# One-hots of every second unit in the last batch: made by ScalarE in two passes in place of VectorE

## The chip, the cores and the metric

One NeuronCore of a Trainium2 chip. The metric is the device time of one execution in microseconds (us). Matrix products run on TensorE (PE in the profile; PEld are its weight loads), elementwise work on VectorE (DVE), ScalarE (ACT) and GpSimd (POOL), and SyncE (SP) issues transfers. Each engine runs its own instructions in program order; between engines there are semaphores only.

## The reference, cut to what matters

Two layers over x (4 batches of 512 tokens, 128 features), each a gated cross attention followed by a gated feed-forward. The change lies in the second layer's attention: for each token, 16 heads and 5 taps per head, a position is computed from the token, and the keys and values of a context of 154 entries are read there by linear interpolation:

```python
ix = ((xg + 1.0) * key_len - 1.0) / 2.0
x0 = jnp.floor(ix);  dx = ix - x0;  i0 = x0.astype(jnp.int32);  i1 = i0 + 1
sk = 0.5 * (w0 * _gather_pad0(Kh, i0) + w1 * _gather_pad0(Kh, i1))
sv = 0.5 * (w0 * _gather_pad0(Vh, i0) + w1 * _gather_pad0(Vh, i1))
scores = jnp.einsum('bhqd,bhqkd->bhqk', Qh / math.sqrt(HD), sk)
attn = jax.nn.softmax(scores, axis=-1)
ctx = jnp.einsum('bhqk,bhqkd->bhqd', attn, sv)
```

## The kernel before, in words

The gather is done by matrix products: positions are turned into one-hot matrices, and a table of keys and values (TAB) is multiplied by them. A batch has 20 units, u0 to u19: four quads of four heads, five taps each (a unit is one quad and one tap; `u // 5` is the quad). Batch b's unit u has the running number i = 20 b + u.

For a unit, SyncE's `load_unit` copies the positions of four heads and 512 tokens, repeated over 128 partitions, into one of four slots of `JBM` (512 KB). A slot is loaded anew when TensorE is through with the unit four before (`g_ready`); the load of u+3 is issued in piece G1.u. VectorE's `onehot` compares the slot with the partition's number (0 to 127) and writes 0 or 1 over it: 128x2048 bf16 to fp16, in place (L1054). Context entries above 127 have a second one-hot for a whole quad, `OHR` (L1052), made with the quad's first unit. TensorE then runs 32 and 8 matmuls into a bank of RING (two banks, taken in turn; L949, L954). ScalarE copies the values out (GV, L688), and VectorE, when that is done, multiplies the keys, still in RING, with the queries (prod, L1374); this frees the bank.

The order of all engines is written out by hand in one list of pieces (ORDER); each engine goes through it and takes its part of each piece. In the list a piece is `kind.batch.number`. G0e starts a batch's gather (first loads, first one-hot). In G1.u VectorE makes the one-hot of **u+1** and then the product of u; with u4, u9, u14 and u19 it also sums the quad's products (dots, L1379). G2a, G2b and G2c are the attention: maximum (VectorE), Exp (ScalarE, L701), sum and weights (VectorE from L1400), weighting of GV (VectorE, L1411 to L1416). In batches 0 to 2 they run once behind all units, in the last batch (batch 3) once for each quad, between the units. G3a to G3d are the projections behind a batch's attention: transposes, an eviction by ScalarE (L584) and a product through the one bank MISC, the addition to x by VectorE (L1034), a layer norm (L1017 to L1025), and, for G3d, the store of the batch by SyncE (L491), which is issued when the last addition is done. Batch 2's lie between the units of batch 3:

```
G0e.3 G1.3.0-3 G3a.2 G1.3.4 G2a.3.0 G3b.2 G1.3.5 G2b.3.0 G1.3.6 G2c.3.0 G1.3.7 G3c.2
G1.3.8-9 G2a.3.1 G3d.2 G1.3.10 G2b.3.1 G1.3.11 G2c.3.1 G1.3.12-14 G2a.3.2 G1.3.15
G2b.3.2 G1.3.16 G2c.3.2 G1.3.17-19 G2a.3.3 G2b.3.3 G2c.3.3 Z0.0-1 ...
```

Z0 to Z3 are the last batch's projections and store, in two halves. Before the last gather ScalarE's part of G0e is empty, and its part of G1.u is the copy of GV alone.

Of the kernel before, what the change touches and what calls it, by code (L numbers as in the profile page):

```python
# [8 lines left out]
ALU = mybir.AluOpType  # L9
# [12 lines left out]
NK = 5  # L22
# [64 lines left out]
def build(nc, x, ctxT, mask, maskT, kmask, gates, consts, wq, wk, wv, wo, bq_col, bk_col, rows,  # L87
# [9 lines left out]
    with ctx:  # L97
# [239 lines left out]
        jb_in = [sem(f"jb_in{i}") for i in range(RINGS)]  # L337
        jbr_in = [sem(f"jbr_in{i}") for i in range(2)]
        oh_ready = sem("oh_ready")
        g_ready = sem("g_ready")  # L340
        gv_ready = sem("gv_ready")
        gk_used = sem("gk_used")
# [19 lines left out]
        def of_quad(a, quad, n):  # L362

            return a[:, :, quad * n:(quad + 1) * n]

        def gathered(i, kv):

# [190 lines left out]
        def _(act):  # L558
# [22 lines left out]
            def evacuate(use, dst, src, bias=0.0):  # L581

                act.wait_ge(misc_ready, use + 1)
                act.activation(dst, src, ACT.Identity, bias=bias).then_inc(misc_free, 1)  # L584

            def lower_read(piece):

                if n := before(piece, "F0a"):
                    act.wait_ge(xl_ready, n)

            for piece in schedule:
                kind, b = piece[0], piece[1]
                m = misc_at[piece]
                if kind == "W":

                    act.wait_ge(lg_ready, 1)
                    act.activation(lg[:, 3, :], lg[:, 2, :], ACT.Exp, accum_out=lg1[:, 1:2]).then_inc(act_done, 1)
                    act.wait_ge(act_done, 1)
                    act.activation(lg1[:, 2:3], lg1[:, 1:2], ACT.Ln)
                    act.activation(lg[:, 4, :], lg[:, 1, :], ACT.Ln).then_inc(act_done, 1)  # L600
                    act.wait_ge(act_done, 2)
                    act.activation(lg[:, 5, :], lg[:, 4, :], ACT.Ln, scale=-1.0).then_inc(noise_ready, 1)
                elif kind == "S":

                    e = 3 * b
                    if b == 2:
                        act.wait_ge(w1_ready, 1)
                        act.dma_start(w1f[0], w1[e:e + 3].rearrange("e d i -> d e i")).then_inc(ld_w1[0], 16)
                    act.wait_ge(ld_w1[b % 2], 16 * (b // 2 + 1))
                    act.activation(W1[:, 0, e:e + 3], w1f[b % 2], ACT.Identity, scale=W1SCALE).then_inc(w1h_ready, 1)  # L610
                elif kind == "A0a":
                    lower_read(piece)
                    evacuate(m, xnT[:], MISC[:])
                elif kind == "A0b":
                    if b == 0:
                        load_rest()
                elif kind in ("G0a", "G3a", "G3c"):
                    evacuate(m, QpTs[b], MISC[:])
                elif kind == "A3":

                    f, u = piece[2:]
                    i = b * AU + f * 5 + u
                    act.wait_ge(st_ready, i + 1)
                    if i >= PS:
                        act.wait_ge(pv_done, (i - PS) // 5 + 1)
                    act.activation(PTs[i % PS], RING[:, i % 2, :], ACT.Exp).then_inc(p_ready, 1)  # L626
                elif kind == "A4a":

                    n = b * 4 + piece[2]
                    act.wait_ge(pv_done, n + 1)  # L630
                    if n:
                        act.wait_ge(ctx_ready, n)
                    act.activation(OT[:], SUM[:], ACT.Identity).then_inc(ot_ready, 1)
                elif kind == "A5a":
                    lower_read(piece)
                    evacuate(m, cxT[:], MISC[:])
                elif kind == "F0a":
                    evacuate(m, xnT[:], MISC[:])
                    act.wait_ge(misc_free, m + 1)
                    act.activation(xnTf[:, b % 2, 0], xnT[:], ACT.Identity).then_inc(xh_ready, 1)  # L640
                elif kind == "F0c":

                    act.wait_ge(misc_free, m + 1)
                    act.activation(gt[:, 1], gt[:, 0], ACT.Exp).then_inc(ex_out, 1)
                elif kind == "F0g":
                    act.wait_ge(d_ready, b + 1)
                    act.activation(gs[:, 6], gs[:, 5], ACT.Exp, scale=0.5).then_inc(ex_out, 1)
                elif kind == "F0d":
                    evacuate(m, w9T[:], MISC[0:NE, :])
                elif kind == "F1" and piece[2] < NE:  # L650
                    e, c = piece[2:]
                    if b == 0 and e == 0 and c == 0:

                        act.wait_ge(kparts_out, 64)
                        act.wait_ge(w1_ready, 3)
                        act.wait_ge(ld_moe, 16 * LD_MOE)
                    i = (b * NE + e) * NC + c
                    act.wait_ge(up_ready, i + 1)
                    if i >= HS:
                        act.wait_ge(down_ready, down_count(i - HS))  # L660
                    act.activation(hT[:, i % HS, :], UP[:, i % 2, :], ACT.Silu,  # L661
                                   bias=b1[:, e, c:c + 1], scale=1.0 / W1SCALE).then_inc(h_ready, 1)
                elif kind == "G0b":
                    act.wait_ge(ld_l1, 16 * 5)
                    act.wait_ge(misc_ready, m + 1)
                    for t in range(NT):
                        last = act.activation(Qxs[b][:, t].rearrange("p (h w d) -> p h w d", h=H, w=2),
                                              MISC[:, t * D:(t + 1) * D].rearrange("p (h d) -> p h d", d=DK).unsqueeze(2)
                                              .broadcast_to((128, H, 2, DK)), ACT.Identity)
                    last.then_inc(misc_free, 1)  # L670
                    evacuate(m + 1, QpTs[b], MISC[:], bias=bcol[:, 2:3])
                elif kind == "G0d":
                    if b >= 1:
                        act.wait_ge(j_out, 16 * b)
                        act.wait_ge(jt_out, 16 * NK * b)
                    act.wait_ge(misc_ready, m + 1)
                    act.activation(jT[:], MISC[0:HN, :], ACT.Identity).then_inc(jT_ready, 1)
                    act.wait_ge(jT_ready, b + 1)
                    act.nop().then_inc(misc_free, 1)
                elif kind == "G1":  # L680
                    u = piece[2]
                    i = b * UN + u
                    if u == 0 and b >= 1:

                        act.wait_ge(cx1_ready, b)
                    act.wait_ge(g_ready, i + 1)
                    quad, n = divmod(u, NK)
                    act.activation(GV[:, n, :, quad * 64:(quad + 1) * 64].rearrange("p t (m d) -> p t m d", d=DK),  # L688
                                   gathered(i, 1), ACT.Identity).then_inc(gv_ready, 1)
                elif kind in ("Z0", "Z2"):  # L690
                    n = b + (2 if kind == "Z2" else 0)
                    act.wait_ge(half_turned, n + 1)
                    act.activation(QpTs[B - 1][:, b * 256:(b + 1) * 256], (UP, DOWN)[n // 2][:, b, 0:256],
                                   ACT.Identity).then_inc(half_read, 1)
                elif kind == "G2b":
                    part = piece[2]
                    sc = scs[b].rearrange("p (x h) -> p x h", h=H)
                    if b == B - 1:
                        sc = of_quad(sc, part, 4)
                    act.wait_ge(z_ready, b + part + 1)  # L700
                    act.activation(sc, sc, ACT.Exp, scale=1.0 / math.sqrt(DK)).then_inc(e_ready, 1)  # L701
# [3 lines left out]
        def _(pe):  # L705
# [49 lines left out]
            for piece in schedule:  # L755
# [178 lines left out]
                elif kind == "G1":  # L934
# [4 lines left out]
                    if u == 0:  # L939

                        pe.wait_ge(p_ready, before(piece, "A3"))
                    pe.wait_ge(oh_ready, i + 1)
                    if i >= 2:
                        pe.wait_ge(gk_used, i - 1)
                    o = RING[:, i % 2, :].rearrange("p (t j c) -> p t j c", t=NT, j=NQ)
# [51 lines left out]
        def _(dve):  # L997
# [47 lines left out]
            def onehot(i):  # L1045

                b, u = divmod(i, UN)
                if u % NK == 0:

                    k = i // NK  # L1050
                    dve.wait_ge(jbr_in[k % 2], 64 * (k // 2 + 1))
                    dve.tensor_scalar(OHR[:, k % 2], JBR[:, k % 2], cst[:, C_KR:C_KR + 1], None, ALU.is_equal)  # L1052
                dve.wait_ge(jb_in[i % RINGS], 16 * (i // RINGS + 1))
                dve.tensor_scalar(OHM[:, i % RINGS], JBM[:, i % RINGS], cst[:, C_K0:C_K0 + 1], None,  # L1054
                                  ALU.is_equal).then_inc(oh_ready, 1)
# [503 lines left out]
```

## Time and profile before

| | us |
|---|---|
| median of 3 runs | 831.93 (830.88 to 833.39) |
| the profiled execution | 831.65 |
| its span in the profile | 829.6 |
| busy: PE, DVE, ACT, POOL | 594.7, 487.7, 244.0, 42.7 |

A span is the time from the first to the last instruction of the profile; the execution's time has some 2 us around it. The last batch's gather with its four attentions begins at about 745 us and ends at 817; the last 12.6 us are the Z pieces. In the profile, GV and the Exp of batch 3 are ScalarE's only steady work there; RING is the bank into which a unit's matmuls go, OHA the tile that holds JBM, OHM and OHR, and QAf, in the last batch, the tile of its weights and scores.

### The profile page before, as it was taken

The page shows a single profiled execution, that of the slowest core. Times are in us where ns is not written, and L with a number is a line of the kernel's source. Part 1 is how long each engine was busy: PE and PEld are TensorE (multiplying, and loading weights), DVE is VectorE, ACT ScalarE, POOL GpSimd, SP SyncE. Part 2 cuts the span into 40 slices and gives each one's busy share as a digit, 9 for nine tenths or more (in the row PEclk, how much of TensorE's full clock was granted, in tenths as well). Part 3 has the DMA queues.
Part 4 walks back from the last instruction along what each step waited for, and adds up shares of the span by engine and source line. Part 5 has one row for each costly group of instructions (what it writes and reads, how often), then busy time and mean ns, then how long its engine had stood idle before and what let it go on. Part 6 is the DMA issues. An engine that isn't in the chain of part 4 may idle for free.

```text
span 829.6 us, 14684 instructions
## 1 busy us (share of the span) xinstructions
PE 594.7 (72%) x6038; PEld 418.9 (50%) x6038; DVE 487.7 (59%) x1173; ACT 244.0 (29%) x421; POOL 42.7 (5%) x52
## 2 busy tenths in 40 slices
PE   2256575968998699777777597988759998406563
PEld 1223122635376478653264486854428887405452
DVE  5736664544136635589446545687255475597765
ACT  0001352304555233204434232315335332201110
POOL 1700000000001100000002000000000000000000
PEclk9977696989999889799998897999979999757655
DMA  3390100210000268710000379300002684058440
GB/s 92 62 305 12 50 2 0 50 20 13 1 1 1 50 160 239 214 53 6 0 21 1 72 252 259 132 5 1 13 0 70 207 231 140 1 142 262 111 143 13
DMA packets 40354, 70.71 MB, mean 85 GB/s; under 512 B 9824, under 2 KB 26577, under 8 KB 40097
## 3 DMA queue, kind: packets, MB, share of 16 engines
q1 hardware_dynamic: 30796, 63.64, 27.6%
q10 hardware_dynamic: 9492, 6.14, 2.6%
q8 instruction: 48, 0.79, 0.4%
q14 instruction: 18, 0.14, 0.1%
HBM read 65.82 MB, written 3.95 MB: 84 GB/s over the span
## 4 chain that ended last, share of the span: by engine, by line
PE 49%; DVE 27%; DMA 9%; issue 6%; ACT 5%; SPq 2%; POOL 1%; POOLq 0%; DVEq 0%; ACTq 0%
PE DOWN L750 12%; PE UP L913 9%; PE RING L949 5%; PE RING L954 3%; DMA OHA<-scratch_positions 3%; DVE nmax L1240 3%; PE MISC L715 2%; PE RING L821 2%; DVE xn L1025 2%; PE MISC L724 2%; DMA OHA<-scratch_q_parts 2%; DVE OHA L1054 2%; DMA QAf<-scratch_q_parts 2%; DVE dots L1379 1%; DVE GV L1441 1%
## 5 line engine op out<-in xcount | busy, mean ns | idle before, releaser
L750 PEld LDWEIGHTS DOWN<-W,hT 128*128 128x128 f32 x1152 | 154.1, 197 | 21.9 <-issue 2.6
L750 PE MATMUL DOWN<-W,hT 128*128 128x128 f32 x1152 | 154.8, 280 | 0.2 <-ACT hT L661 0.2
L661 ACT ACTIVATE hT<-UP,b 128x512 f32<-128x512 f32 x144 | 98.3, 687 | 158.9 <-PE UP L913 158.5
L913 PE MATMUL UP<-xnTf,W 128*128 128x512 f16 x432 | 124.3, 403 | 3.4 <-ACT hT L661 3.0
L949 PE MATMUL RING<-TAB,OHA 128*128 128x32 f16 x2560 | 78.8, 180 | 53.6 <-DVE OHA L1054 32.4
L949 PEld LDWEIGHTS RING<-TAB,OHA 128*128 128x128 f16 x2560 | 74.4, 99 | 61.6 <-DVE OHA L1054 39.0
L688 ACT ACTIVATE GV<-RING 128x256 f32<-128x256 f32 x80 | 30.7, 383 | 149.9 <-PE RING L954 149.9
L1070 DVE SCALAR_TENSOR_TENSOR acc<-DOWN,W,acc 128x128 f32<-128x128 f32 x128 | 36.0, 344 | 59.6 <-PE DOWN L750 53.1
L1054 DVE TENSOR_SCALAR OHA<-OHA,cst 128x2048 f16<-128x2048 bf16 x80 | 59.5, 748 | 13.4 <-DMA OHA<-scratch_positions 12.7
L1240 DVE TENSOR_REDUCE nmax<-RING 128x3 f32<-128x462 f32 (+1 forms) x96 | 53.7, 585 | 19.2 <-PE RING L824 15.1
L913 PEld LDWEIGHTS UP<-xnTf,W 128*128 128x128 f16 x432 | 42.4, 103 | 35.2 <-issue 9.5
L954 PE MATMUL RING<-TAB,OHA 128*128 128x128 f16 x640 | 58.8, 247 | 0.0
L1374 DVE TENSOR_TENSOR prod<-RING,Qx 128x256 f32<-128x256 f32 x60 | 25.4, 423 | 53.1 <-ACT GV L688 52.9
L515 POOL TENSOR_TENSOR rstd<-ve,mhalf 128x4 f32<-128x4 f32 x15 | 15.1, 1008 | 717.4 <-DVE ve L1022 717.4
L954 PEld LDWEIGHTS RING<-TAB,OHA 128*128 128x128 f16 x640 | 44.4, 110 | 0.0
L626 ACT ACTIVATE PT<-RING 128x512 f32<-128x512 f32 x54 | 30.9, 600 | 32.0 <-PE SUM L737 15.6
L715 PE MATMUL MISC<-cst,xn 128*128 128x128 f32 x60 | 12.7, 350 | 36.8 <-DVE xn L1025 36.8
L821 PE MATMUL RING<-mb,identb 128*128 128x462 bf16 (+1 forms) x72 | 28.1, 390 | 13.2 <-DVE nmax L1240 7.9
L1025 DVE TENSOR_SCALAR xn<-X,mv,rstd 128x128 f32<-128x128 f32 x60 | 23.0, 558 | 17.0 <-POOL rstd L515 17.0
L715 PEld LDWEIGHTS MISC<-cst,xn 128*128 128x128 f32 x60 | 8.7, 176 | 40.7 <-DVE xn L1025 28.4
L846 PE MATMUL RING<-mbM,identb 128*128 128x512 bf16 x48 | 19.5, 406 | 12.8 <-DMA QAf<-scratch_max_parts 6.8
L824 PE MATMUL RING<-KA,QAf 128*128 128x154 bf16 x192 | 28.0, 254 | 0.0
(321 smaller groups left out, 774.2 us busy)
## 6 DMA issues: line engine op xcount, KB each, us to landing
OHA<-scratch_positions SPq DMA_DIRECT2D x80, 512.0 KB, 5.6
OHA<-scratch_tail_positions SPq DMA_DIRECT2D x48, 160.0 KB, 4.9
OHA<-scratch_positions SPq DMA_DIRECT2D x16, 160.0 KB, 3.9
QAf<-scratch_q_parts SPq DMA_DIRECT2D x18, 128.0 KB
hT<-in_w ACTq DMA_DIRECT2D x3, 768.0 KB, 6.1
W<-in_w ACTq DMA_DIRECT2D x3, 768.0 KB
scratch_q_parts<-qs SPq DMA_DIRECT2D x4, 384.0 KB, 2.5
X<-in_x ACTq DMA_DIRECT2D x4, 256.0 KB, 4.9
```

What stands on the lines that cost most here:

```text
L626: act.activation(PTs[i % PS], RING[:, i % 2, :], ACT.Exp).then_inc(p_ready, 1)
L661: act.activation(hT[:, i % HS, :], UP[:, i % 2, :], ACT.Silu, bias=b1[:, e, c:c + 1], scale=1.0 / W1SCALE).then_inc(h_ready, 1)
L715: last = pe.transpose(MISC[0:width, t * 128:(t + 1) * 128], src[:, t, :], ident)
L750: last = pe.matmul(DOWN[:, n % 2, t * 128:(t + 1) * 128], hT[:, (k + c) % HS, t * 128:(t + 1) * 128], W2[:, e, c, :], start=(c == 0), stop ...
L821: pe.matmul(o, identb[:], mb[:, t, :].unsqueeze(1).broadcast_to((128, n, S2)), start=True, stop=False)
L913: last = pe.matmul(UP[:, i % 2, :], W1[:, pw, e, c * 128:(c + 1) * 128], xnTf[:, b % 2, px], start=(n == 0), stop=(n == 2))
L949: pe.matmul(o[:, t, j, :], OHM[:, i % RINGS, j, t * 128:(t + 1) * 128], TAB[:, b, 0, part, quad * NQ + j, :], start=((j, t, part) == (0, 0 ...
L954: last = pe.matmul(o[:, t], OHR[:, (b * NQ + quad) % 2, n, t * 128:(t + 1) * 128], TAB[:, b, 1, part, quad * NQ:(quad + 1) * NQ, :], start ...
L1025: last = dve.tensor_scalar(xn[:, t, :], X[:, b, t, :], mv[:, t, 0:1], rstd[:, t:t + 1], ALU.subtract, ALU.mult)
L1054: dve.tensor_scalar(OHM[:, i % RINGS], JBM[:, i % RINGS], cst[:, C_K0:C_K0 + 1], None, ALU.is_equal).then_inc(oh_ready, 1)
L1070: last = dve.scalar_tensor_tensor(out=acc[:, t, :], in0=o, scalar=W9[:, b % 2, t, e:e + 1], in1=acc[:, t, :], op0=ALU.mult, op1=ALU.add)
L1240: dve.tensor_reduce(nmax[:, h:h + n, t], RING[:, i % 2, 0:n * S2].rearrange("p (h k) -> p h k", h=n), AX.X, ALU.max, negate=True).then_inc ...
```

## The change

In the last batch the one-hot of the odd units (u1, u3, ... u19) is made by ScalarE, in two passes over the slot, both in place: |k - position|, then max(0, 1 - that), which is 1 where the position is the partition's number and 0 elsewhere. ScalarE makes u1's in G0e.3 and that of u+2 in G1.u, right behind the copy of u's values. VectorE leaves out these units and keeps the tails (`OHR`) of all quads. TensorE waits for ScalarE's count as well as for VectorE's, and for a count of the tails whose unit is ScalarE's (u5, u15).

```diff
+        def on_act(i):
+            return i >= (B - 1) * UN and i % UN % 2 == 1
...
+            def act_onehot(i):
+                n = sum(on_act(k) for k in range(i + 1))
+                act.wait_ge(jb_in[i % RINGS], 16 * (i // RINGS + 1))
+                act.activation(JBM[:, i % RINGS], JBM[:, i % RINGS], ACT.Abs, bias=cst[:, C_K0:C_K0 + 1],
+                               scale=-1.0).then_inc(oh_dist, 1)
+                act.wait_ge(oh_dist, n)
+                act.activation(OHM[:, i % RINGS], JBM[:, i % RINGS], ACT.Relu, bias=1.0, scale=-1.0).then_inc(oh_act, 1)
...
                     act.activation(GV[:, n, :, quad * 64:(quad + 1) * 64].rearrange("p t (m d) -> p t m d", d=DK),
                                    gathered(i, 1), ACT.Identity).then_inc(gv_ready, 1)
+                    if u + 2 < UN and on_act(i + 2):
+                        act_onehot(i + 2)
+                elif kind == "G0e" and b == B - 1:
+                    act_onehot(b * UN + 1)
...
-                    pe.wait_ge(oh_ready, i + 1)
+                    given = sum(on_act(k) for k in range(i + 1))
+                    pe.wait_ge(oh_ready, i + 1 - given)
+                    if given:
+                        pe.wait_ge(oh_act, given)
+                    if tails := sum(on_act(k) for k in range(0, i + 1, NK)):
+                        pe.wait_ge(oh_tail, tails)
...
-                    dve.tensor_scalar(OHR[:, k % 2], JBR[:, k % 2], cst[:, C_KR:C_KR + 1], None, ALU.is_equal)
+                    tail = dve.tensor_scalar(OHR[:, k % 2], JBR[:, k % 2], cst[:, C_KR:C_KR + 1], None, ALU.is_equal)
+                    if on_act(i):
+                        tail.then_inc(oh_tail, 1)
+                if on_act(i):
+                    return
                 dve.wait_ge(jb_in[i % RINGS], 16 * (i // RINGS + 1))
```

## Rows read from the trace of the kernel before

**Rows 1.** Busy time by stretch: engines (instructions), granted clock, DMA share, GB/s.

```profile
740.00:760.00 20.00, 10.52 (x253) 9.75 (x253) 15.83 (x24) 3.16 (x8) 0.00 (x0) 0.76 0.82 252
...
780.00:800.00 20.00, 10.76 (x240) 9.37 (x240) 15.97 (x33) 2.48 (x7) 0.00 (x0) 0.58 0.78 231
```

**Rows 2.** ScalarE's waits, 745 to 817: total us, times, longest.

```profile
ACT GV L688 <- PE RING L954: 57.6, 20, 17.2
```

**Rows 3.** Chain of waits, 744 to 817: start, us; first and last one-hot of seven.

```profile
752.91 0.76 DVE OHA L1054
...
780.68 0.51 SPq L388
...
803.92 0.68 DVE OHA L1054
```

**Rows 4.** ScalarE's instructions grouped by shape, whole execution: busy us, mean ns.

```profile
L584 ACT ACTIVATE QpT<-MISC 128x512 f32<-128x512 f32 x9 | 5.4, 595 | 11.0 <-PE MISC L715 11.0
L610 ACT ACTIVATE W<-hT 128x1536 f16<-128x1536 f32 x3 | 4.3, 1472 | 23.3 <-DMA hT<-in_w 23.3
L701 ACT ACT_TABLE_LOAD x3 | 3.8, 1283 | 0.1
...
L640 ACT ACTIVATE xnTf<-xnT 128x512 f16<-128x512 f32 x4 | 2.5, 630 | 0.1
...
L584 ACT ACTIVATE QpT<-MISC,bcol 128x512 f32<-128x512 f32 x3 | 2.1, 688 | 3.6 <-PE MISC L926 3.6
```

**Rows 5.** DMA issues at 734.8 (u1) and 780.7 us (u13): last number, us to landing.

```profile
OHA<-scratch_positions SPq DMA_DIRECT2D x1, 512.0 KB, 8.3
OHA<-scratch_positions SPq DMA_DIRECT2D x1, 512.0 KB, 5.7
```

**Rows 6.** ScalarE's timeline: GV of u1, u3; G3a's eviction; u4, u5; Exp; u9, u13.

```profile
749.54 0.38 ACT L688 ACTIVATE GV<-RING 128x256 f32<-128x256 f32 x1 [1.14 <-PE RING L954]
...
752.56 0.38 ACT L688 ACTIVATE GV<-RING 128x256 f32<-128x256 f32 x1 [1.07 <-PE RING L954]
753.00 0.60 ACT L584 ACTIVATE QpT<-MISC 128x512 f32<-128x512 f32 x1
755.18 0.38 ACT L688 ACTIVATE GV<-RING 128x256 f32<-128x256 f32 x1 [1.58 <-PE RING L954]
757.54 0.38 ACT L688 ACTIVATE GV<-RING 128x256 f32<-128x256 f32 x1 [1.98 <-PE RING L954]
758.89 0.27 ACT L701 ACTIVATE QAf<-QAf 128x80 f32<-128x80 f32 x1 [0.96 <-DVE QAf L1390]
...
775.74 0.38 ACT L688 ACTIVATE GV<-RING 128x256 f32<-128x256 f32 x1 [1.32 <-PE RING L954]
...
789.66 0.38 ACT L688 ACTIVATE GV<-RING 128x256 f32<-128x256 f32 x1 [3.98 <-PE RING L954]
```

**Rows 7.** TensorE's timeline: first 32 matmuls of u3 and of u13.

```profile
751.10 0.97 PE L949 MATMUL RING<-TAB,OHA 128*128 128x32 f16 x32
...
787.73 1.03 PE L949 MATMUL RING<-TAB,OHA 128*128 128x32 f16 x32 [2.48 <-DVE OHA L1054]
```

**Rows 8.** VectorE's timeline: products of u4, u6, u10, u14, u16 (L1374); sums (L1400).

```profile
755.60 0.42 DVE L1374 TENSOR_TENSOR prod<-RING,QAf 128x256 f32<-128x256 f32 x1
...
760.55 0.28 DVE L1400 TENSOR_REDUCE sm<-QAf 128x16 f32<-128x80 f32 x1
...
762.70 0.42 DVE L1374 TENSOR_TENSOR prod<-RING,QAf 128x256 f32<-128x256 f32 x1
...
780.98 0.42 DVE L1374 TENSOR_TENSOR prod<-RING,QAf 128x256 f32<-128x256 f32 x1
...
793.81 0.42 DVE L1374 TENSOR_TENSOR prod<-RING,QAf 128x256 f32<-128x256 f32 x1 [0.61 <-ACT GV L688]
...
797.97 0.28 DVE L1400 TENSOR_REDUCE sm<-QAf 128x16 f32<-128x80 f32 x1
...
800.12 0.42 DVE L1374 TENSOR_TENSOR prod<-RING,QAf 128x256 f32<-128x256 f32 x1 [0.16 <-ACT GV L688]
```

More of the change, by code:

```diff
@@ L339, in build @@
         oh_ready = sem("oh_ready")
+        oh_tail = sem("oh_tail")
+        oh_dist = sem("oh_dist")
+        oh_act = sem("oh_act")
         g_ready = sem("g_ready")
```

## The prediction, made before the changed kernel ran

> **What bounds the kernel now.** I read the busy time by stretch first, then the chain of waits from 744 us to the end, then ScalarE's waits and the two engines' timelines. All times here are of the one profiled execution: span 829.6 us, 831.65 us as timed. The change touches nothing before the last batch's gather, its 20 units (u0 to u19) between 745 and 809 us and the four quads' attention between them.
>
> In that stretch no engine is full, but VectorE comes nearest: 15.97 of 20 us, against 2.48 for ScalarE and 10.76 for TensorE [rows 1]. ScalarE waits 57.6 us in the gather for TensorE's units [rows 2]. So there is room on ScalarE by the sum. The chain says where time is lost: it runs through VectorE's one-hot, the unit's 40 matmuls, ScalarE's eviction of the values (GV), VectorE's product, then the quad's attention and the next one-hot. Seven of the 20 one-hots are on it, the first and the last at 752.91 and 803.92 [rows 3]. Counting one-hots along VectorE's order, these seven belong to u4, u6, u8, u10, u14, u16 and u18: **every one is an even unit**. The odd units' one-hots, the ones that the change takes off VectorE, run while VectorE would wait for a GV, or for a transfer.
>
> **What goes.** Ten one-hots of 0.68 to 0.76 us [rows 3] leave VectorE: about 7 us of work, and by the chain none of it on the path. I take 0 for it, except in three places where the product behind it becomes early enough to matter once others are late; they are in the steps below.
>
> **What comes.** Ten times two ScalarE passes over 128x2048 16-bit values, in ScalarE's program order. The trace shows no Abs or Relu. Nearest rows, SBUF to SBUF: 128x512 takes 630 ns, 128x1536 takes 1472 ns [rows 4], so 0.82 ns per column and 1472 + 512 x 0.82 = 1.89 us for 2048 columns. A bias held in a column adds 0.09 us (688 against 595 ns [rows 4]): an estimate of 1.98 us for a pass. The ends: 0.75 us, if ScalarE did the tile as fast as VectorE [rows 3], and four times 630 ns = 2.52 us. I take 1.98, since the 1472 ns row is by far the nearest in length and writes 16 bits too. A pair is then 3.95 us from the eviction before to the instruction behind, the passes' small overlaps and the wait between them counted as nothing.
>
> The Trainium skill (ScalarE: Activation LUTs, "What ACT_TABLE_LOAD costs") says that an activation costs the same per element in fp32 and bf16. These rows read fp32 and no row reads 16 bits, so they neither bear it out nor deny it. By its 0.833 ns a column and 280 ns the pass would be an estimate of 1.99 us, and the sum +11; were the rule wrong and 16 bits ran at half the cost, it would be the first rival's 833.3.
>
> **What is behind the pair.** This decides. The pair for u+2 stands behind GV(u), u odd, and ahead of whatever ScalarE does next: GV(u+1), on which VectorE's product of that unit waits, the eviction for batch 2's last projections, and the quads' Exp. Step by step, before -> after:
>
> u1: its load, 8.3 us to land [rows 5], and its passes run while VectorE still weights batch 2. Nothing; otherwise u1's matmuls would start later than u0's end.
>
> u3: GV(1) ends at 749.92 [rows 6], passes to 753.87. TensorE's u3 goes from 751.10 [rows 7] to 753.9. It takes 1.42 us, so GV(3) 752.56 -> 755.36 [rows 6], ends 755.74.
>
> u5: passes to 759.7. Behind them stands the eviction for G3a.2, 753.00 -> 759.7, and behind that GV(4), 755.18 -> 760.3 [rows 6]. The product of u4, 755.60 -> 760.7 [rows 8]: **+5.1**. The same eviction frees MISC for G3b.2, which stands ahead of u5 in TensorE's order, so GV(5) goes from 757.54 [rows 6] to about 763.4 with matmuls at their present rate, 764 if the longer gaps leave TensorE at 1.2 GHz (its granted clock is 0.76 of 2.4 GHz over 740 to 760 us, and 0.58, so mostly the lower level, over 780 to 800 [rows 1]).
>
> u7: passes from 764.0 to about 767.8, and the Exp of quad 0 behind them, 758.89 -> 767.8 [rows 6]. VectorE needs it at its sum of quad 0, 760.55 -> 768.0 [rows 8]; now it had been early. Four instructions later, without u7's one-hot, comes the product of u6, 762.70 -> 769.25 [rows 8]: **+1.45 more, 6.55**.
>
> u9: the load and the passes lie beside quad 0's last sums and the layer norm. Nothing; all of that moves by 6.55.
>
> u11: GV(9) 775.74 [rows 6] + 6.55 ends at 782.7, passes to 786.6, GV(10) 787.0. Product of u10 780.98 -> 787.05 [rows 8], **6.05**: VectorE gets back 0.5 since u11's one-hot stood ahead of that product.
>
> u13: its load is issued behind batch 2's store, at 780.68 [rows 3], 787.25 after, and lands 5.7 us later [rows 5], 792.95. ScalarE stands at it with GV(12) queued behind, passes to 796.9. TensorE's u13 787.73 [rows 7] -> 796.95, and takes 1.9 us (GV(13) at 789.66 [rows 6]).
>
> u15: GV(13) ends 799.25, passes to 803.2, GV(14) behind them to 803.6. Product of u14 793.81 -> 803.6 [rows 8]: **9.8**.
>
> u17: TensorE's u15 803.2 to 805.1, GV(15) to 805.5, passes to 809.45, Exp of quad 2 to 809.75. Its sum 797.97 -> 809.75; the product of u16 800.12 -> 811.0 [rows 8], u17's one-hot being gone from between: **10.9**.
>
> u19: passes end about 815.8, TensorE reaches u19 at 817.4. Nothing. The tail moves as it stands.
>
> **Sum:** 5.1 + 1.45 - 0.5 + 3.75 + 1.1 = +10.9 us. 831.65 + 10.9 = 842.6; the median of before is 831.93, 0.28 above its profile, so 842.8, and I say 843. Twelve passes lie on the path (u3, u5, u7, u13, u15, u17), so 0.1 us a pass is 1.2 us. With 2.52 us a pass it is 10.9 + 12 x 0.54 = +17.4, and some more as u19 is then late too: 850. With 0.75 us the same steps leave only the G3a eviction and GV(4) 0.6 late: 832.5.
>
> **Rivals.**
> 1. 16-bit passes run at half the cost, 1.0 us. Pair 2.05: u3 0.9 late, GV(4) 1.3 late, Exp of quad 0 just in time, u13's passes over at 789.75 and GV(14) no later than the rest. +1.3: 833.3. For: VectorE's one-hot shows that a 16-bit tile can be quick; against: the 16-bit output of the 1472 ns row brought ScalarE nothing visible.
> 2. **Faster.** VectorE is the bound at 80% busy, ScalarE's 57.6 idle us take the pairs, and the released one-hots come off the path: ten of 0.67 us, 831.9 - 6.7 = 825.2. The place is VectorE's order in quads 0 to 2. It decides where a pair is done before GV(u+1) is due; GV(1) and GV(3) are 3.0 us apart [rows 6], so GV(2) is due some 1.5 us behind GV(1), and a pass must stay below about 0.7 us. Against: the chain has no odd one-hot, and 1.98 is far off.
> 3. Abs or Relu needs another table than Exp: a load of 1.28 us [rows 4] to Exp and one back. Exp of quads 0 to 3 would each be 1.28 later, 4 x 1.28 = 5.1, 848. For: no row has Abs or Relu. Against: the Exp line has three loads in the whole execution [rows 4] for its seven Exps, one in each batch before the last and four here, and Identity stands between all of them. The Trainium skill (ScalarE: Activation LUTs, "Table sets: the hidden batching unit") has relu and abs in every set; no run so far shows it. By that rule there is no load, and the sum stays.
> 4. The pairs vanish in ScalarE's idle time and nothing moves: 832. It needs GV(4) and Exp of quad 0 with 4 us of slack; GV(4) has none [rows 8].
>
> **How the numbers follow.** Forecast 0.78, with its own range 838 to 848 (passes of 1.75 to 2.2 us, loads 1 to 2 us off, TensorE's level). Rival 1 0.07, rival 2 0.03, rival 3 0.05, rival 4 0.03; 0.04 for waits longer than I see, above 850. A measurement tells 0.3%, 2.5 us, from no change. Within it are rival 4 and rival 1 but for 0.01 in which that one comes out above 834.4: 0.09. Rival 2 is the faster case, 0.03; the rest is slower, 0.88. The range 836 to 850 holds the forecast and rival 3 and leaves out the rest, 0.17.
>
> **What would show it.** Right: Abs and Relu at about 2 us each; u3's matmuls start behind ScalarE instead of VectorE; the eviction for G3a.2 at about 760; VectorE waits for Exp in quads 0 and 2, some 2 us each; u13's Abs waits for its load; GV ahead of a product becomes VectorE's chief wait; the tail behind the last quad unchanged but some 11 us later. Wrong: passes near 1 us, a table load beside Exp, an odd one-hot's removal that moves a product earlier, or a time below 836.

## The result: slower, and the profile after

The changed kernel takes 847.74 us (842.62 to 851.62) against 831.40 of before on the same chip: a ratio of 1.0178, interval 1.0146 to 1.0211. In a second comparison it took 844.73 against 833.64: 1.0125, interval 1.0076 to 1.0173. That is 16 and 11 us more, where 11 were predicted.

These totals scatter by several us, so the stretch that the change touches is the better measure: from u0's first matmul to the end of quad 3's weighting. Its two ends, before (TensorE's and VectorE's timeline: start, duration, line):

```profile
746.06 1.02 PE L949 MATMUL RING<-TAB,OHA 128*128 128x32 f16 x32 [21.06 <-issue]
...
816.70 0.29 DVE L1416 TENSOR_TENSOR QAf<-GV 128x128 f32<-128x128 f32 x1
```

and after:

```profile
752.11 1.01 PE L974 MATMUL RING<-TAB,OHA 128*128 128x32 f16 x32 [21.06 <-issue]
...
834.81 0.29 DVE L1445 TENSOR_TENSOR QAf<-GV 128x128 f32<-128x128 f32 x1
```

The stretch took 816.99 - 746.06 = **70.93 us** and takes 835.10 - 752.11 = **82.99 us: 12.06 more**. Another 6.05 us of this execution lie ahead of it, where both programs do the same. One piece of that shows between 410 and 445 us: TensorE's granted clock there was 0.95 before, nearly all at 2.4 GHz, and 0.81 after, where it got through 132 matmuls in place of 159 (busy time by stretch, columns as in [rows 1]); before, then after:

```profile
410.00:445.00 35.00, 26.00 (x159) 18.44 (x160) 19.45 (x86) 14.25 (x21) 3.02 (x3) 0.95 0.05 13
```

```profile
410.00:445.00 35.00, 25.05 (x132) 17.22 (x125) 17.52 (x75) 11.96 (x17) 3.02 (x3) 0.81 0.05 13
```

In a second profile of the changed kernel u0 starts at 745.73, as early as before, and the stretch is 82.71.

The busy time of the stretch (columns as in [rows 1]), before and then after:

```profile
746.06:816.99 70.93, 37.88 (x826) 34.30 (x826) 54.67 (x113) 9.94 (x26) 1.01 (x1) 0.62 0.51 151
```

```profile
752.11:835.10 82.99, 40.45 (x826) 36.80 (x826) 48.27 (x103) 43.51 (x45) 1.01 (x1) 0.56 0.42 129
```

VectorE (the third engine) has 6.4 us less to do and ScalarE (the fourth) 33.6 us more. VectorE's instructions themselves take as long as before: a one-hot 747 ns against 749, a product 422 in both.

The two new passes and the table loads of the Exp line, among ScalarE's groups of the changed kernel (busy us, mean ns | idle before, releaser), against [rows 4]:

```profile
L704 ACT ACTIVATE GV<-RING 128x256 f32<-128x256 f32 x80 | 30.6, 382 | 115.6 <-PE RING L979 115.6
L597 ACT ACTIVATE OHA<-OHA,cst 128x2048 bf16<-128x2048 bf16 x10 | 19.9, 1994 | 16.6 <-DMA OHA<-scratch_positions 16.6
L600 ACT ACTIVATE OHA<-OHA 128x2048 f16<-128x2048 bf16 x10 | 19.1, 1910 | 0.3
...
L721 ACT ACT_TABLE_LOAD x3 | 3.8, 1283 | 0.1
```

Abs takes 1.99 us, Relu 1.91, and there are three table loads as before. Their places, in ScalarE's timeline after (against [rows 6]):

```profile
755.72 0.39 ACT L704 ACTIVATE GV<-RING 128x256 f32<-128x256 f32 x1 [1.26 <-PE RING L979]
756.00 1.99 ACT L597 ACTIVATE OHA<-OHA,cst 128x2048 bf16<-128x2048 bf16 x1
758.02 1.91 ACT L600 ACTIVATE OHA<-OHA 128x2048 f16<-128x2048 bf16 x1
759.84 0.36 ACT L704 ACTIVATE GV<-RING 128x256 f32<-128x256 f32 x1
761.94 0.39 ACT L704 ACTIVATE GV<-RING 128x256 f32<-128x256 f32 x1 [1.73 <-PE RING L979]
762.22 1.99 ACT L597 ACTIVATE OHA<-OHA,cst 128x2048 bf16<-128x2048 bf16 x1
764.24 1.91 ACT L600 ACTIVATE OHA<-OHA 128x2048 f16<-128x2048 bf16 x1
766.06 0.58 ACT L591 ACTIVATE QpT<-MISC 128x512 f32<-128x512 f32 x1
766.53 0.38 ACT L704 ACTIVATE GV<-RING 128x256 f32<-128x256 f32 x1
770.75 0.38 ACT L704 ACTIVATE GV<-RING 128x256 f32<-128x256 f32 x1 [3.84 <-PE RING L979]
771.03 1.99 ACT L597 ACTIVATE OHA<-OHA,cst 128x2048 bf16<-128x2048 bf16 x1
773.05 1.91 ACT L600 ACTIVATE OHA<-OHA 128x2048 f16<-128x2048 bf16 x1
774.87 0.25 ACT L721 ACTIVATE QAf<-QAf 128x80 f32<-128x80 f32 x1
```

The reader is to look at the lines **without** a bracket: GV(2), the eviction L591, GV(4) and the Exp L721 wait for nobody but ScalarE itself; they stand in its order behind a pair. Before, each of them had a bracket or stood directly behind one: it waited for its data.

VectorE's waits in the stretch (line, waited for: total us, times, longest), before and then after:

```profile
DVE prod L1374 <- ACT GV L688: 8.9, 8, 2.7
DVE OHA L1054 <- DMA OHA<-scratch_positions: 3.6, 2, 2.6
...
DVE sm L1400 <- ACT QAf L701: 0.3, 1, 0.3
```

```profile
DVE prod L1403 <- ACT GV L704: 26.3, 11, 4.6
DVE sm L1429 <- ACT QAf L721: 5.3, 3, 3.2
```

VectorE waits 17.4 us more for GV and 5.0 more for Exp; the 3.6 us of waits for loads are gone.

### The profile page after: what moved, and what is told of

The parts are those of the page before. It is cut to its first block, busy times and chain, and to the rows that moved or that the text cites. A ratio compares the mean times of both kernels' runs of the same rounds, so it can differ in the third digit from the quotient of the medians.

```text
span 847.9 us, 14709 instructions
## 1 busy us (share of the span) xinstructions
PE 600.1 (71%) x6038; PEld 423.1 (50%) x6038; DVE 480.9 (57%) x1163; ACT 281.0 (33%) x441; POOL 42.7 (5%) x52
## 4 chain that ended last, share of the span: by engine, by line
PE 48%; DVE 25%; DMA 9%; ACT 7%; issue 7%; SPq 2%; POOL 1%; POOLq 0%; DVEq 0%; ACTq 0%
PE DOWN L770 12%; PE UP L933 9%; PE RING L974 5%; PE RING L979 4%; DVE nmax L1269 3%; DMA OHA<-scratch_positions 3%; PE MISC L735 2%; PE MISC L744 2%; PE RING L841 2%; DVE xn L1050 2%; DMA OHA<-scratch_q_parts 2%; DMA QAf<-scratch_q_parts 2%; DVE GV L1470 1%; DVE OHA L1083 1%; PE RING L844 1%
## 5 line engine op out<-in xcount | busy, mean ns | idle before, releaser
L933 PEld LDWEIGHTS UP<-xnTf,W 128*128 128x128 f16 x432 | 42.6, 104 | 37.4 <-issue 10.2
L1083 DVE TENSOR_SCALAR OHA<-OHA,cst 128x2048 f16<-128x2048 bf16 x70 | 52.1, 748 | 11.7 <-DMA OHA<-scratch_positions 11.3
L642 ACT ACTIVATE PT<-RING 128x512 f32<-128x512 f32 x54 | 30.9, 600 | 31.7 <-PE SUM L757 15.6
L735 PE MATMUL MISC<-cst,xn 128*128 128x128 f32 x60 | 12.4, 343 | 37.8 <-DVE xn L1050 37.8
## 6 DMA issues: line engine op xcount, KB each, us to landing
hT<-in_w ACTq DMA_DIRECT2D x3, 768.0 KB, 6.3
W<-in_w ACTq DMA_DIRECT2D x3, 768.0 KB
```

Of the source, the lines that this page charges most:

```text
L735: last = pe.transpose(MISC[0:width, t * 128:(t + 1) * 128], src[:, t, :], ident)
L933: last = pe.matmul(UP[:, i % 2, :], W1[:, pw, e, c * 128:(c + 1) * 128], xnTf[:, b % 2, px], start=(n == 0), stop=(n == 2))
```

## The experiments

Each was timed beside the kernel before on one chip; "stretch" is that of its profile, as above. The kernel before has 70.93 and, in a second profile, 70.36; 70.65 is taken as its value.

**The two kernels again.** No edit.

> The changed kernel once more, unchanged. Its profile was 6.05 us late before u0's first matmul, where the programs do the same, and 12.06 us slower from u0's first matmul to the end of quad 3's weighting (70.9 to 83.0 us). Theory A (the cost is what stands behind ScalarE's pairs in the gather; the rest is the spread of earlier stages): that stretch is 83.0 again within 0.5 us, and u0's first matmul is somewhere between 742 and 754. Theory B (the change also slows the stages before it): u0 is again at 750 or later.

Measured: stretch 82.71, u0's first matmul at 745.73; 1.0125.

> The kernel before, unchanged, for its spread. The stretch from u0's first matmul to the end of quad 3's weighting 70.9 us again within 0.5 us; time 1.000 of before within 0.3%. Theory A: u0's first matmul moves by some us between profiles (746.06 in the first), and so the 6 us ahead of it in the changed kernel's profile are of this kind. Theory B: it stays at 746 within 1 us.

Measured: stretch 70.36, a little outside the 0.5 us expected; u0 at 744.39; ratio 0.999 (0.9953 to 1.0027). So two profiles of one kernel differ by 0.6 us in the stretch, and a difference of that size between single profiles says nothing in what follows. Over the 13 profiles of this study u0's first matmul lies between 742.3 and 752.1, the first profile of the changed kernel being the latest. With the 745.73 of the second profile that speaks for theory A: the 6 us ahead of the stretch are scatter, and the change costs 12.

**What VectorE's odd one-hots were worth.**

```diff
-                    if given:
-                        pe.wait_ge(oh_act, given)
+                    if on_act(i):
+                        pe.wait_ge(jb_in[i % RINGS], 16 * (i // RINGS + 1))
...
-                        act_onehot(i + 2)
...
-                    act_onehot(b * UN + 1)
```

> What VectorE's ten one-hots are worth: the odd units of the last batch get no one-hot at all (left out: their positions go to TensorE as they are), ScalarE has no passes, TensorE waits for the load. Theory A (no odd one-hot is on the path): the stretch stays at 70.9 us within 0.7, no faster. Rival (VectorE is the bound): ten times 0.67 us less, 64 us, time 0.992 of before.

Measured: stretch 71.59, ratio 0.9989 (0.9961 to 1.0017). Nothing is gained by taking ten one-hots away altogether. VectorE's waits in this kernel show where the time of the ten one-hots went:

```profile
DVE prod L1399 <- ACT GV L704: 14.9, 10, 3.3
DVE OHA L1079 <- DMA OHA<-scratch_positions: 5.5, 2, 4.3
```

6.0 us more waiting for GV and 1.9 more for loads: the freed time is waiting time. The rival with the gain falls.

**ScalarE's passes alone, read by nobody.**

```diff
-                act.activation(JBM[:, i % RINGS], JBM[:, i % RINGS], ACT.Abs, ...
+                spare = PT4[:]. ... .bitcast(BF16)[:, 0:NQ * S] ...
+                act.activation(spare, W1[:, 0, 0:NQ], ACT.Abs, ...
                 act.wait_ge(oh_dist, n)
-                act.activation(OHM[:, i % RINGS], JBM[:, i % RINGS], ACT.Relu, ...
+                act.activation(spare, spare, ACT.Relu, ...
+                act.wait_ge(oh_act, n)
...
-                if on_act(i):
-                    return
```

> What ScalarE's passes cost by standing in its order alone: VectorE makes all one-hots as before, ScalarE runs the same ten pairs of passes with the same waits in the same places, but into a tile that nobody reads. Theory A (what stands behind the pairs decides): most of the loss stays, as the evictions and Exp are as late as before, without the odd units' matmuls being late: 7 to 9 us, the stretch 78 to 80 us. Rival (the odd units' one-hots are late, 4 us instead of 0.75, and nothing else): 70.9 us, time as before.

Measured: stretch 80.83, 10.2 more; ratio 1.0105 (1.0069 to 1.0141). Most of the loss is there although every one-hot comes from VectorE as before. It is above the 7 to 9 expected. Three things in this kernel's ScalarE timeline were not counted there. The edit has one wait more than the changed kernel: ScalarE also waits for the end of its own Relu, so from GV(1) to GV(2), with u3's pair between, it takes 4.25 us here against 4.12 in the changed kernel, 0.13 us a pair. And u5's pair waits 0.45 us and u15's 0.94 us for their loads:

```profile
750.24 0.38 ACT L705 ACTIVATE GV<-RING 128x256 f32<-128x256 f32 x1 [1.24 <-PE RING L975]
...
754.49 0.66 ACT L705 ACTIVATE GV<-RING 128x256 f32<-128x256 f32 x2
755.60 2.00 ACT L598 ACTIVATE PT<-W,cst 128x2048 bf16<-128x2048 f16 x1 [0.45 <-DMA OHA<-scratch_positions]
...
794.48 2.00 ACT L598 ACTIVATE PT<-W,cst 128x2048 bf16<-128x2048 f16 x1 [3.64 <-DMA OHA<-scratch_positions]
...
800.05 2.00 ACT L598 ACTIVATE PT<-W,cst 128x2048 bf16<-128x2048 f16 x1 [0.94 <-DMA OHA<-scratch_positions]
```

With six pairs on the path that is up to 0.45 + 0.94 + 6 x 0.13 = 2.2 us, as much as the result lies above the middle of the expectation; that all of it is on the path is not shown. Without the extra waits, at most 0.8 us, 9.4 of the 12 are still there.

**Which pairs cost.** The set of odd units is replaced:

```diff
-            return i >= (B - 1) * UN and i % UN % 2 == 1
+            return i >= (B - 1) * UN and i % UN in (1, 9, 11, 19)
```

> ScalarE makes the one-hots of u1, u9, u11 and u19 alone, VectorE the rest. These are the pairs behind which, by theory A, nothing due stands (u11 alone; with the others late VectorE lost nothing by it). Theory A: four pairs, 16 us of ScalarE, cost nothing: the stretch 70.4 to 71.6 us. Rival (each pair costs its share, a tenth of 12 us): 4.8 us more, 75.4 us.

Measured: stretch 71.24, ratio 0.9996 (0.9967 to 1.0024). Four pairs, 15.6 us of ScalarE, cost nothing that can be told. In its timeline u9's pair is over well before the next eviction's data. GV(10), behind u11's pair, comes 33.70 us after u0's first matmul against 32.50 before: it is late, but VectorE comes to that product without u11's one-hot, and nothing is lost that can be told:

```profile
767.44 1.91 ACT L600 ACTIVATE OHA<-OHA 128x2048 f16<-128x2048 bf16 x1
772.10 0.60 ACT L591 ACTIVATE QpT<-MISC 128x512 f32<-128x512 f32 x1 [2.75 <-PE MISC L735]
...
779.64 0.36 ACT L704 ACTIVATE GV<-RING 128x256 f32<-128x256 f32 x1
```

> The other six: u3, u5, u7, u13, u15 and u17 by ScalarE, VectorE the rest. Theory A: all of the loss, 10 to 12 us, the stretch 81 to 83 us. Rival (each pair costs its share): 7.2 us more, 78 us.

Here `(3, 5, 7, 13, 15, 17)`. Measured: stretch 83.03, ratio 1.0140 (1.0083 to 1.0197). The six have all of the loss; a share for each pair would have been 7.

**The same six in their groups**, `(3, 5)`, `(7, 17)` and `(13, 15)`:

> The prediction's steps one group at a time. ScalarE makes u3 and u5 alone. Predicted for this step: 5.1 us (the eviction for G3a.2 and GV(4) behind the pairs). Theory A: the stretch 75.5 to 76.6 us (70.4 to 70.9 before, plus 5.1 to 5.7). Rival (a share for each pair): 73.3 us.

Measured: stretch 76.38, 5.7 more; 1.0075 (1.0049 to 1.0102).

> ScalarE makes u7 and u17 alone, the pairs ahead of the Exp of quads 0 and 2. Predicted for these steps: 1.45 + 1.1 = 2.5 us, with u5 and u15 late before them. Alone, GV(5) and GV(15) come early and the Exp has more time: 1.5 to 2.6 us, the stretch 72 to 73.5 us. Rival (a share for each pair): 73.3 us, not to be told apart here; what tells is where VectorE waits: theory A has it wait for Exp in quads 0 and 2 and nowhere else more than before.

Measured: stretch 72.72, 2.1 more; 1.0038 (1.0010 to 1.0065). VectorE's waits of this kernel; only that for Exp has grown by more than 1 us:

```profile
DVE prod L1401 <- ACT GV L704: 8.7, 7, 2.7
DVE OHA L1081 <- DMA OHA<-scratch_positions: 4.2, 2, 3.0
DVE sm L1427 <- ACT QAf L719: 3.2, 3, 1.5
```

> ScalarE makes u13 and u15 alone: u13's load comes late behind batch 2's store, and GV(12) and GV(14) stand behind the pairs. Predicted for this step: 3.75 us. Theory A: 3.3 to 4.0 us, the stretch 73.7 to 74.9 us. Rival (a share for each pair): 73.3 us.

Measured: stretch 73.54, 2.9 more, below the 3.3 expected; 1.0046 (1.0021 to 1.0072). By its size alone it fits the rival's 73.3 better; what speaks for theory A here is the timeline. It shows the step as predicted, the wait for u13's load with GV(12) behind the pair:

```profile
787.07 2.00 ACT L597 ACTIVATE OHA<-OHA,cst 128x2048 bf16<-128x2048 bf16 x1 [3.14 <-DMA OHA<-scratch_positions]
789.11 1.91 ACT L600 ACTIVATE OHA<-OHA 128x2048 f16<-128x2048 bf16 x1
790.92 0.36 ACT L704 ACTIVATE GV<-RING 128x256 f32<-128x256 f32 x1
```

The groups sum to 10.7 us, against 12.4 for the six together. Each is one profile, and four stretches that may each be off by 0.6 us could make up the difference; whether groups that follow one another cost more than alone is not shown.

**Half the passes.**

```diff
-                act.activation(JBM[:, i % RINGS], JBM[:, i % RINGS], ACT.Abs, ...
-                act.wait_ge(oh_dist, n)
```

> All odd units by ScalarE, with the second pass alone (left out: the distance, so the values are no one-hots). Theory A: a pair of half the length fits better into the gaps, and Exp, the eviction and GV are hardly late: 2 to 3 us more than before, the stretch 73 to 74 us. Rival (the loss goes with ScalarE's added busy time): half of 12, 76.9 us.

Measured: stretch 71.36, 0.7 more, even less than expected; 0.9996 (0.9966 to 1.0026). Half of ScalarE's added time, a seventeenth of the loss: what counts is how far a pair overruns the gap it stands in, not its length. In its timeline GV(4), behind a pass and the eviction, starts 9.98 us after u0's first matmul (745.80), against 9.12 before and 14.42 with both passes:

```profile
753.49 1.91 ACT L597 ACTIVATE OHA<-OHA 128x2048 f16<-128x2048 bf16 x1
755.31 0.58 ACT L591 ACTIVATE QpT<-MISC 128x512 f32<-128x512 f32 x1
755.78 0.37 ACT L701 ACTIVATE GV<-RING 128x256 f32<-128x256 f32 x1
```

**A version from these results.** The chain of before had even units on it, so the pairs are given to three of them, `(6, 8, 18)`.

> ScalarE makes u6, u8 and u18 alone, right behind the GV of u4, u6 and u16, and VectorE the rest. These one-hots are on the chain of before: VectorE comes to them late, behind a quad's attention, with the load long landed and ScalarE idle. Theory A: TensorE's u6, u8 and u18 start 0.3 to 0.7 us earlier each: the stretch 69.3 to 70.9 us, time 0.998 to 1.000 of before, perhaps not to be told from it. Rival (any pair on ScalarE costs about 1.2 us): 74.5 us, 1.004.

Measured: stretch 70.11, 0.25 to 0.8 less than the two of before; ratio 0.998 (0.9951 to 1.0008). No loss, and if there is a gain it cannot be told from none. Counted from u0's first matmul, u6 starts 0.09 us earlier than in the first profile of before, u8 0.39 and u18 0.66. For u6 the reason given does not hold: its load had not long landed, and its pair waits for it:

```profile
755.29 2.00 ACT L597 ACTIVATE OHA<-OHA,cst 128x2048 bf16<-128x2048 bf16 x1 [0.99 <-DMA OHA<-scratch_positions]
```

## Why the prediction was right

The time, 847.74 in the first comparison, is in the range, and slower was right, by the steps named. It lies 4.7 us above the 843, the second comparison's 844.73 lies 1.7 above; the first profile has 6.05 us of scatter ahead of the stretch. In the stretch 10.9 us stand against 12.06. Each step, as moved from before to after; the after times of the first profile are lowered by the 6.05 us at which u0 starts later:

| step | predicted | measured |
|---|---|---|
| Abs, Relu | 1.98 each | 1.99, 1.91 |
| u3's first matmul, 751.10 -> | 753.9 | 753.98 |
| GV(3), 752.56 -> | 755.36 | 755.89 |
| G3a's eviction, 753.00 -> | 759.7 | 760.01 |
| product of u4, 755.60 -> | 760.7 | 760.89 |
| GV(5), 757.54 -> | 763.4 to 764 | 764.70 |
| sum of quad 0, 760.55 -> | 768.0 | 769.10 |
| product of u6, 762.70 -> | 769.25 | 770.36 |
| product of u10, 780.98 -> | 787.05 | 787.97 |
| u13's Abs, behind its load | 792.95 | 794.37 |
| product of u14, 793.81 -> | 803.6 | 804.83 |
| sum of quad 2, 797.97 -> | 809.75 | 810.94 |
| product of u16, 800.12 -> | 811.0 | 812.19 |
| end of the stretch, + | 10.9 | 12.06 |

By the products of u4, u6, u10, u14 and u16 the measured sum is 5.29 + 2.37 - 0.67 + 4.03 + 1.05 = 12.07 us, against 5.1 + 1.45 - 0.5 + 3.75 + 1.1. What was mis-sized is mainly one piece, TensorE's time between u3 and quad 0's sum, and with it the second term: 1.1 us too little there, and from then on the lag stays at 0.9 to 1.2 (1.4 at u13's load, which took 6.0 us in place of 5.7). The chain of waits after shows that piece (start, us, what):

```profile
760.03 1.02 PE RING L974 x32
761.05 0.87 PE RING L979 x8
...
766.69 0.61 PE MISC L741
767.30 1.71 PE MISC L744 x8
769.01 0.85 PE RING L974 x32
769.86 0.87 PE RING L979 x8
```

u3's matmuls are 1.89 us here; the prediction took 1.42, their length before, when TensorE had come to them without a gap. After, it idles 2.91 us before u3 and 2.23 before G3b. The busy time of the stretch from u2 to u6's start, before, and of that from u3 to u7's start, after, has the granted clock in its third number from the right:

```profile
749.65:760.36 10.71, 7.07 (x174) 6.45 (x174) 8.61 (x16) 2.67 (x7) 0.00 (x0) 0.96 0.88 282
```

```profile
760.03:775.10 15.07, 10.38 (x175) 9.40 (x176) 7.14 (x13) 9.43 (x11) 0.00 (x0) 0.50 0.58 169
```

0.96 and 0.50: nearly all at 2.4 GHz before, all at 1.2 after. It is 0.47 us on u3; 0.31 of it is left at the eviction, since a pair takes 4.12 us from the start of the GV before it to the instruction behind it (761.94 to 766.06), where the prediction has 4.33 and no overlap. GV(5) is 0.70 behind the 764 that was allowed for the lower level, so G3b and u5 took 0.4 more than that. The last 0.3 is a slip of the prediction, which lets u7's passes begin at 764.0, when a GV that starts then is not yet through. So the gaps that a late one-hot makes seem to be paid twice: over the whole stretch the same 826 matmuls keep TensorE busy for 40.45 us in place of 37.88, at a granted clock of 0.56 in place of 0.62. That the clock is the reason is read from these rows; no run held it fixed.

The groups run alone bear out the first terms: 5.7 and 2.1 us against 5.1 and 1.45 + 1.1. The third, 2.9 against 3.75, was given a wrong size for a run by itself. In the sum 3.75 also takes back the 0.5 that VectorE gained at u11, because u13's load, which starts the step, moves by the whole 6.55. Alone, by the prediction's own times, the load lands at 786.4, u13's passes end at 790.3 and u15's at 796.6, and the product of u14 goes from 793.81 to 797.0: 3.2 us.

That the odd one-hots were worth nothing, the step read from seven even units on the chain, is shown by the kernel without them.

Rival 1 falls with the passes' 1.99 and 1.91 us. Its price was of the right size: with one pass of 1.91 us in place of its pair of 2.05, the stretch is 0.7 longer against its 1.3, and GV(4) 0.86 late against its 1.3. Relu has its bias in the instruction, so the 1.89 us that the prediction worked out without a column is its estimate, against 1.91. The Trainium skill (ScalarE: Activation LUTs, "What ACT_TABLE_LOAD costs") has activations at one rate in fp32 and bf16, 1.99 us as an estimate for Abs; the trace agrees with 1994 ns. Rival 3 falls with the three loads; that relu and abs are in every set, as the Trainium skill says (ScalarE: Activation LUTs, "Table sets: the hidden batching unit"), agrees with that. Rival 4 falls with the stretch, rival 2 with the kernel without the odd one-hots. The prediction's 57.6 us of waiting on ScalarE hold one wait of 17.2 that ends at 748.02, most of it ahead of u0; but ScalarE waits for others too, and in the stretch it is busy for 9.94 of 70.93 us, so there is as much room as it says.

The signs named ahead were there, with one that reads otherwise than said: the wait for a one-hot from ScalarE is shown mostly as "issue", not as ScalarE's, and only u15's has ScalarE's name. The wait of 2.91 us before u3 is ScalarE's all the same; u3's first matmul starts 0.1 us after the end of L600 at 759.93. VectorE waits 3.17 us for the Exp of quad 0 and 1.84 for that of quad 2.

## What to carry to other kernels

Work moved to an idle engine is priced by the instruction that stands behind it in that engine's order, not by the engine's idle sum: ScalarE was idle for 61 of the stretch's 71 us and 39 us of passes cost 12, though four of the ten pairs cost nothing. Before moving work off a busy engine, look which instances of it are on the chain of waits: here only the even ones were, and the odd ones were moved. And a pair that fits into its gap is free while one twice as long is not, so halving a moved piece can take away nearly all of its cost.

## What was not expected of the hardware

The time of the stages before u0, which all these programs share, scatters by up to 10 us between executions (u0 at 742.3 to 752.1 in 13 profiles; at 752.1 and 745.7 in two of the changed kernel), of which one piece was seen to go with TensorE's granted clock (0.95 against 0.81 over 410 to 445 us). A comparison of stretches between two events in the profiles settled to 0.6 us what the totals gave to 3 or 4.
